# Expert stage of a fused perceiver kernel: sums copied to the output ahead of the last scatter, a narrower 16-bit table, an earlier plan, and a reordered middle stage

## The chip, the cores and the metric

The kernel is one program on one core of a Trainium2 chip. The metric is the device time of one execution in microseconds; lower is better. Times are medians of three executions. A change of 0.2% is about what such a measurement can tell from no change.

## The reference, cut to what matters

The input is x (32 sequences of 32 tokens, 1024 tokens of width 512) and a context of 32 x 257 rows of width 384. Six residual layers follow each other: a cross attention, an attention, a low-rank expert layer, a second cross attention, an attention without softmax, and a mixture of experts. The last one is what most of the change touches:

```python
# _L1_ffn_ref, per token t of 1024, 8 experts, 2 chosen
probs = softmax(x @ router_w.T)
top_w, top_idx = top_k(probs, 2); top_w /= sum(top_w)
g, u = x @ wg[e].T, x @ wu[e].T          # 512 -> 1024
out[t] = sum over the chosen e of  top_w * ((silu(g) * u) @ wd[e].T)
return x + out
```

## The kernel before

The program runs six stages one after the other, each a function with its own block of code for every engine and a barrier of all engines behind it: `latents`, `cross0`, `middle`, `cross1`, `poly`, `experts`. Every product of matrices is three 16-bit matmuls (lines 106 to 108: high by high, high by low, low by high), so most operands exist as a high and a low half. ScalarE writes the high half, VectorE or GpSimd the low one.

**middle** (attention and low-rank experts) walks 8 tiles of 128 tokens through 11 slots of a software pipeline. In slot s the lanes are t = s (output projection, residual, norm a, q/k/v), b = s-1 (softmax and attention, norm b), q = s-2 (gates, low-rank product, norm q) and last = s-3 (next stage's query). The order on each engine is written out by hand in its loop over s, and an engine works strictly in that order. The steps used below: `residual_o(t)` adds the projection to X and takes statistics (L1351 to L1346); `power` on GpSimd makes the reciprocal root (L1309, L1311); `scale` on ScalarE writes the normed row (L1496); `bias_o(t+1)` on GpSimd adds a row of biases to the next tile of X (L1314); `turned_high`, `turned_low` copy a transposed tile into halves (L1500, L1356); `soft`, `soft_exp`, `soft_scale`, `soft_high`, `soft_low` are the softmax of b (L1376 to L1392); `gates`, `gates_end` and `down` are q's gates and the scaled low-rank row dg (L1168 to L1194, L1413).

**cross1** starts with four fills on GpSimd (L1762, L1764). `sig.begin` raises counters at a loop's start so that the first pass finds its waits met; here it gives the counter d_xlo on which TensorE's first `keys` waits.

**experts** first works out a plan on all partitions alike: how many tokens each expert has, how many tiles of 128 (`tiles`, cast into `plan`), and from it a table of tiles by tokens. The table has TABLE = 34 columns (MOST = 24 possible tiles, 8, and 2). VectorE makes `past`, `inside`, three planes of `entries` and the one-hot `lane`; TensorE multiplies them into PSUM in 16 matmuls; VectorE turns the result into `fromtab`, `totab` and `gtab` (row to read, row to add into, weight). GpSimd gathers the first tile's rows, TensorE turns them (L2864), and the walk over the experts begins.

In the walk each engine reads two numbers of the plan per expert (`number`, L2579: its tiles and its first tile) and branches. Per tile TensorE makes four groups of gate and up products (pGU), turns the next tile's rows, and makes the down product (pY) of 24 matmuls. The run of the profile has 21 tiles: 2, 3, 3, 2, 3, 3, 3, 2 per expert. Expert weights come as 12 pieces of 1024 columns through a ring of 12 buffers. ScalarE writes a piece's high half (L2805), VectorE its low half (`split`, L2663), and the split's counter e_wlo lets SyncE load the next expert's piece into the buffer and lets TensorE start an expert once 12 are there. During an expert's first two tiles the next expert's pieces are split, 6 per tile: 2 ahead of the groups and one after each group.

A tile's result is weighted (`outputs`) and added by GpSimd's indirect transfer into the scratch tensor `sums` in DRAM one tile later. At the end the last result is scattered, its landing awaited, and `sums` is copied to the output.

## Time and profile before

| | before |
|---|---|
| median of three executions | 1804.37 us (1803.74 to 1806.03) |
| the profiled execution, its own time | 1802.4 us |
| its span, first to last instruction | 1800.7 us |
| mean granted clock of TensorE | 0.94 |
| TensorE, VectorE, ScalarE, GpSimd busy | 87%, 70%, 55%, 38% |

The span is what the profiler sees; 1.7 us of the execution's own time lie around it. Where a row names idle time, it is the time in which that engine did nothing just ahead of that instruction, and the name behind the arrow is who ended it. A granted clock of 1.00 is 2.4 GHz for TensorE, 0.50 is 1.2 GHz.

### The profile page before, as it was taken

Reading aid. Unit: us, or ns where it says so; the run is one execution under the profiler, and the core shown is the slowest. Engines: PE = TensorE matmul, PEld = TensorE weight load, DVE = VectorE, ACT = ScalarE, POOL = GpSimd, SP = SyncE. Lnnn points to the kernel's source line nnn. Section 1 sums busy time; section 2 is a strip of 40 time slices with the busy share of each in tenths; the row PEclk is TensorE's granted clock in tenths of the full one; section 3 lists DMA queues with packets and bytes.
Section 4 is the critical chain, followed back from the end, with each engine's and each line's share of the span. In section 5 each row is a group of like instructions: output and inputs, shape, how many; then the busy total and the mean of one; then the engine's idle time right before and its main releaser. Section 6 shows DMA issues by size and latency. Waiting matters only on the chain. (4 is left out here: it accounts for less than half of the span.)

```text
span 1800.7 us, 43529 instructions
## 1 busy us (share of the span) xinstructions
PE 1569.4 (87%) x16191; PEld 1125.5 (63%) x16191; DVE 1255.2 (70%) x2853; ACT 985.1 (55%) x2210; POOL 675.8 (38%) x796
## 2 busy tenths in 40 slices
PE   6968999999857886799999999599992699989996
PEld 3535777777645665577777777245551577777875
DVE  7858998999745777588888887577775754454431
ACT  4547887888633443366666666333333455565541
POOL 4557777777511110212211121245552223332332
PEclk9979999999978998799999999699995799999998
DMA  6111011111140000011110113401002775565422
GB/s 225 45 58 36 28 46 46 46 46 45 34 170 1 2 1 1 19 35 35 35 35 26 35 35 149 149 1 36 13 13 91 220 205 142 145 188 154 119 38 67
DMA packets 50105, 126.95 MB, mean 70 GB/s; under 512 B 6913, under 2 KB 19553, under 8 KB 49889
## 3 DMA queue, kind: packets, MB, share of 16 engines
q1 hardware_dynamic: 44914, 112.64, 19.4%
q0 software_dynamic: 5008, 11.80, 3.4%
q8 instruction: 123, 2.02, 0.5%
q14 instruction: 60, 0.49, 0.1%
HBM read 110.83 MB, written 15.68 MB: 70 GB/s over the span
## 5 line engine op out<-in xcount | busy, mean ns | idle before, releaser
L106 PE MATMUL e_pGU<-XT,WB 128*128 128x128 f16 x1344 | 232.1, 222 | 18.1 <-issue 9.0
L107 PE MATMUL e_pGU<-XT,WB 128*128 128x128 f16 x1344 | 231.9, 222 | 1.1 <-issue 1.1
L108 PE MATMUL e_pGU<-XT,WB 128*128 128x128 f16 x1344 | 231.8, 222 | 0.0
L2663 DVE SCALAR_TENSOR_TENSOR WB<-raw,WB 128x1024 f16<-128x1024 f32 x96 | 115.5, 1223 | 86.0 <-ACT WB L2805 85.9
L106 PEld LDWEIGHTS e_pGU<-XT,WB 128*128 128x128 f16 x1344 | 133.6, 99 | 23.3 <-issue 21.8
L107 PEld LDWEIGHTS e_pGU<-XT,WB 128*128 128x128 f16 x1344 | 133.6, 99 | 1.5
L108 PEld LDWEIGHTS e_pGU<-XT,WB 128*128 128x128 f16 x1344 | 133.6, 99 | 1.3 <-issue 1.3
L2646 POOL TENSOR_TENSOR XT<-e_mf,XT 128x256 f16<-128x256 f32 x84 | 56.2, 669 | 173.6 <-ACT XT L2819 173.6
L1780 POOL TENSOR_TENSOR XT<-dzo,XT 128x128 f32 (+1 forms) x32 | 13.7, 427 | 283.8 <-ACT XT L1921 283.8
L715 POOL TENSOR_TENSOR crn<-css,mhalf 128x8 f32<-128x8 f32 x64 | 108.6, 1697 | 5.3
L2805 ACT ACTIVATE WB<-raw 128x1024 f16<-128x1024 f32 x96 | 97.9, 1044 | 13.5 <-PE e_pY L108 12.5
L2779 DVE SCALAR_TENSOR_TENSOR e_mf<-e_pGU,e_sg 128x256 f32<-128x256 f32 x84 | 35.4, 421 | 84.4 <-ACT e_sg L2817 81.9
L1908 ACT ACTIVATE dpr<-dpS,dnm 128x257 f32<-128x257 f32 x128 | 59.0, 474 | 39.7 <-DVE dnm L1819 39.7
L106 PE MATMUL cpK<-W,cLT 128*128 128x512 f16 x192 | 74.0, 386 | 1.0 <-POOL cLT L704 1.0
L2819 ACT ACTIVATE XT<-e_mf 128x256 f16<-128x256 f32 x84 | 35.0, 417 | 72.0 <-DVE e_mf L2779 72.0
L107 PE MATMUL cpK<-W,cLT 128*128 128x512 f16 x192 | 74.0, 386 | 0.0
L108 PE MATMUL cpK<-W,cLT 128*128 128x512 f16 x192 | 73.9, 385 | 0.0
L106 PE MATMUL cpP<-cPT,raw 128*128 128x128 f16 x384 | 69.2, 222 | 4.8 <-DVE raw L810 2.5
L106 PE MATMUL pl_bM<-W,pl_LT 128*128 128x512 f16 x160 | 61.4, 384 | 9.7 <-DVE pl_LT L2226 9.7
L107 PE MATMUL cpP<-cPT,raw 128*128 128x128 f16 x384 | 68.6, 221 | 0.0
L108 PE MATMUL cpP<-cPT,raw 128*128 128x128 f16 x384 | 68.5, 221 | 0.0
L2817 ACT ACTIVATE e_sg<-e_pGU 128x256 f32<-128x256 f32 x84 | 31.6, 377 | 63.3 <-PE e_pGU L108 62.3
(581 smaller groups left out, 5809.5 us busy)
## 6 DMA issues: line engine op xcount, KB each, us to landing
raw<-in_WE SPq DMA_DIRECT2D x96, 512.0 KB, 4.8
raw<-in_W SPq DMA_DIRECT2D x37, 512.0 KB, 7.5
ctxin<-in_ctx SPq DMA_DIRECT2D x32, 384.0 KB, 3.3
ctxin<-in_ctxT SPq DMA_DIRECT2D x32, 384.0 KB
cv<-vlat SPq DMA_DIRECT2D x32, 96.0 KB
X<-in_x SPq DMA_DIRECT2D x8, 256.0 KB, 8.6
vlat<-vl SPq DMA_DIRECT2D x8, 256.0 KB, 2.0
dv<-vrem SPq DMA_DIRECT2D x128, 0.8 KB
```

The source lines that it names most:

```text
L106: pe.matmul(out, lh, rh, start=first, stop=False, skip_group_check=shared)
L107: pe.matmul(out, lh, rl, start=False, stop=False, skip_group_check=shared)
L108: return pe.matmul(out, ll, rh, start=False, stop=last, skip_group_check=shared)
L715: pool.tensor_tensor(rn[i][:, :], ss[i][:, :], mhalf[:, 0:H0], ALU.pow).then_inc(sig[f"c0_rn{i}"], 1)
L1780: pool.tensor_tensor(dst[:, 1, :, :], zo[:, :, :], dst[:, 0, :, :], ALU.subtract).then_inc(sig["d_olo"], 1)
L1908: act.activation(pr[:, g, :], pS[:, g, 0:SC], ACT.Exp, bias=nm[:, g:g + 1], scale=SCALE, accum_out=rsum[:, g:g + 1]).then_inc(sig["d_exp"], 1)
L2646: pool.tensor_tensor(mT[:, 1, 2 * g:2 * g + 2, :], mf[g % 2][:, :].rearrange("p (a n) -> p a n", a=2), mT[:, 0, 2 * g:2 * g + 2, :], ALU.s ...
L2663: dve.scalar_tensor_tensor(WB[w][:, 1, a], ring[n][:, :], WS, WB[w][:, 0, a], ALU.mult, ALU.subtract)\
L2779: dve.scalar_tensor_tensor(mf[g % 2][:, :], pGU[g % 2][:, 2 * T:4 * T], 1.0 / WS, sg[g % 2][:, :], ALU.mult, ALU.mult)\
L2805: act.activation(WB[w][:, 0, a], ring[n][:, :], ACT.Copy, scale=WS).then_inc(sig["e_whi"], 1)
L2817: act.activation(sg[g % 2][:, :], pGU[g % 2][:, 0:2 * T], ACT.Silu, scale=1.0 / WS).then_inc(sig["e_sg"], 1)
L2819: act.activation(mT[:, 0, 2 * g:2 * g + 2, :], mf[g % 2][:, :].rearrange("p (a n) -> p a n", a=2), ACT.Copy)\
```

## The change

It does seven things: (1) in middle, VectorE's `residual_o` moves two steps ahead and `soft_scale` behind `turned_low`, ScalarE's `turned_high` moves ahead of `soft_exp`, and GpSimd's `bias_o` moves behind the slot's three `power` calls; (2) in cross1 the begin of two counters moves ahead of the fills; (3) the table has 26 columns and its operands are 16-bit; (4) of the first expert's splits on VectorE, 4 move from ahead of the plan and 3 from ahead of the table's result to behind it; (5) TensorE starts the first gate product after 8 pieces, and the other 4 are split inside the first tile; (6) TensorE reads all 16 numbers of the plan ahead of the table; (7) `sums` is copied to the output once every scatter but the last has landed, and the last goes into the output itself, with rows past the end skipped.

```diff
@@ middle, GpSimd
                 if t is not None:
                     power("a", t)
-                    if t + 1 < NT:
-                        bias_o(t + 1)
                 if b is not None:
                     power("b", b)
                 if q is not None:
                     power("q", q)
+                if t is not None and t + 1 < NT:
+                    bias_o(t + 1)
@@ middle, VectorE
                 if q is not None:
                     turned_low("b", q, bT1, LTb)
+                if t is not None:
+                    residual_o(t)
                 if last is not None:
                     turned_low("q", last, bT0, LTq)
...
                 if b is not None:
                     value_low(b)
-                if t is not None:
-                    residual_o(t)
...
                     soft(b)
-                    soft_scale(b)
                 if q is not None:
                     gates_end(sig, dve, "m_g", q, gate[:, :, :], gwork)
                 if t is not None:
                     turned_low("a", t, bT0, LTa)
                 if b is not None:
+                    soft_scale(b)
                     soft_low(b)
@@ middle, ScalarE
-                if b is not None:
-                    soft_exp(b)
                 if t is not None:
                     turned_high("a", t, bT0, LTa)
                 if b is not None:
+                    soft_exp(b)
                     soft_high(b)
@@ cross1, GpSimd
+            sig.begin(pool, "d_olo", "d_xlo")
             for u in range(2):
                 pool.memset(qbd[u][:, :, :, :], 0.0).then_inc(sig["d_const"], 1)
...
-            sig.begin(pool, "d_olo", "d_xlo")
@@ experts
+    GUP = 2 * CK * INTER // PW
+    USED = MOST + 2
...
-                here, ahead = number(eng, e, SLOTS), number(eng, e + E1, MOST)
+                here, ahead = known[e] if known else (number(eng, e, SLOTS), number(eng, e + E1, MOST))
@@ experts, SyncE
+            sp.wait_ge(sig["e_plan"], 1)
+            total = number(sp, 2 * E1, MOST)
+            sp.wait_ge(sig["e_put"], (total + 1) * 16)
+            sp.dma_start(st["out"], sums[0:TOK, :]).then_inc(sig["e_out"], 16)
             sp.wait_ge(sig["e_end"], 1)
-            sp.dma_start(st["out"], sums[0:TOK, :]).then_inc(sig["e_out"], 16)
-            sp.wait_ge(sig["e_out"], 16)
@@ experts, GpSimd
+            pool.wait_ge(sig["e_out"], 16)
             pool.wait_ge(sig["e_y"], total + 1)
             sig.passed(pool, "pool")
-            scatter()
-            pool.wait_ge(sig["e_put"], (total + 2) * 16)
+            pool.indirect_dma_start(st["out"], bass.IndirectOffsetOnAxis(ap=torow[:, 0:1], axis=0), yo[:, :], None, compute_op=ALU.add,
+                                    bounds_check=TOK - 1, oob_is_err=False).then_inc(sig["e_last"], 16)
+            pool.wait_ge(sig["e_last"], 16)
@@ experts, VectorE
-            for n in range(4):
-                split(0, 0, n)
             dve.wait_ge(sig["e_counted"], 1)
...
-            for n in range(4, 8):
-                split(0, 0, n)
+            split(0, 0, 0)
             dve.wait_ge(sig["e_tabled"], 1)
...
+                coming = owed(e, w, pieces) + [(e + 1, 1 - w, n) for n in pieces]
+                for piece in coming[:LATE]:
+                    split(*piece)
...
+                    for piece in coming[LATE + g:LATE + g + 1]:
+                        split(*piece)
+                for piece in coming[LATE + GROUPS:]:
+                    split(*piece)
+
+            def owed(e, w, pieces):
+                return [(e, w, n) for n in range(GUP, PIECES)] if e == 0 and 0 in pieces else []
...
-            for n in range(8, PIECES):
+            for n in range(1, 6):
                 split(0, 0, n)
             dve.wait_ge(sig["e_turned"], 1)
             dve.tensor_copy(xg[:, 1, :, :], pX[1][:, 0:CK * T].rearrange("p (k n) -> p k n", k=CK)).then_inc(sig["e_xlo"], 1)
+            for n in range(6, GUP):
+                split(0, 0, n)
@@ experts, TensorE
+            pe.wait_ge(sig["e_plan"], 1)
+            known = [(number(pe, e, SLOTS), number(pe, e + E1, MOST)) for e in range(E1)]
             pe.wait_ge(sig["e_plans"], 1)
             pe.wait_ge(sig["e_entries"], 3)
...
-                pe.wait_ge(sig["e_wlo"], e * PIECES + PIECES)
+                pe.wait_ge(sig["e_wlo"], e * PIECES + (PIECES if e else GUP))
...
                 pe.wait_ge(sig["e_y"], j + 1)
+                if not e:
+                    pe.wait_ge(sig["e_wlo"], PIECES)
...
-            walk_experts(pe, tile)
+            walk_experts(pe, tile, None, known)
```

VectorE in a full slot of middle, from the value row to the gates' first step (the lines with no sign stand in both kernels):

```order
 L1366 SCALAR_TENSOR_TENSOR mid_zt<-mid_V,mrows 128x512
 L1356 TENSOR_TENSOR mid_LTb<-mid_T,mid_LTb 128x512
-L1356 TENSOR_TENSOR mid_LTq<-mid_T,mid_LTq 128x512
-L1370 TENSOR_TENSOR mid_v<-mid_zt,mid_v 128x512
 L1351 SCALAR_TENSOR_TENSOR X<-mid_O,X 128x512
 L1340 BN_STATS mid_ast<-X 128x6
 L1344 BN_AGGR mid_amv<-mid_ast 128x2
 L1346 TENSOR_SCALAR mid_amv<-mid_amv 128x1
+L1356 TENSOR_TENSOR mid_LTq<-mid_T,mid_LTq 128x512
+L1370 TENSOR_TENSOR mid_v<-mid_zt,mid_v 128x512
```

The residual and its three statistics now stand ahead of the low halves of LTq and v. On GpSimd, two slots of middle:

```order
-L1314 TENSOR_TENSOR X<-X,mrows 128x512
 L1309 TENSOR_TENSOR mid_brs<-mid_bmv,mhalf 128x1
 L1311 TENSOR_SCALAR mid_brs<-mid_brs,mid_bmv 128x1
 L1309 TENSOR_TENSOR mid_qrs<-mid_qmv,mhalf 128x1
 L1311 TENSOR_SCALAR mid_qrs<-mid_qrs,mid_qmv 128x1
+L1314 TENSOR_TENSOR X<-X,mrows 128x512
 L1309 TENSOR_TENSOR mid_ars<-mid_amv,mhalf 128x1
 L1311 TENSOR_SCALAR mid_ars<-mid_ars,mid_amv 128x1
-L1314 TENSOR_TENSOR X<-X,mrows 128x512
 L1309 TENSOR_TENSOR mid_brs<-mid_bmv,mhalf 128x1
 L1311 TENSOR_SCALAR mid_brs<-mid_brs,mid_bmv 128x1
```

The bias add of 128x512 now follows the reciprocal root of q, the last of the slot, where it followed that of a. VectorE at the start of experts, from the last small step ahead of the plan to the transposed rows; before:

```order
L2690 TENSOR_SCALAR r_own<-r_own 128x1
L2663 SCALAR_TENSOR_TENSOR WB<-raw,WB 128x1024 x4
L2694 COPY e_count<-e_pR 128x8
...
L2731 TENSOR_TENSOR e_entries<-e_inside,e_values 128x16x34 x3
L2734 TENSOR_TENSOR XT<-r_count,e_within 128x2048
L2663 SCALAR_TENSOR_TENSOR WB<-raw,WB 128x1024 x4
L2740 COPY e_token<-e_pR 128x34
...
L2752 SCALAR_TENSOR_TENSOR e_gtab<-e_pR,e_gtab 128x34
L2663 SCALAR_TENSOR_TENSOR WB<-raw,WB 128x1024 x4
L2793 COPY XT<-e_pX 128x512
```

and with the change:

```order
L2697 TENSOR_SCALAR r_own<-r_own 128x1
L2699 COPY e_count<-e_pR 128x8
...
L2736 TENSOR_TENSOR e_entries<-e_inside,e_values 128x16x26 x3
L2741 TENSOR_TENSOR XT<-e_numbers,e_within 128x1024 x2
L2669 SCALAR_TENSOR_TENSOR WB<-raw,WB 128x1024
L2747 COPY e_token<-e_pR 128x26
...
L2759 SCALAR_TENSOR_TENSOR e_gtab<-e_pR,e_gtab 128x26
L2669 SCALAR_TENSOR_TENSOR WB<-raw,WB 128x1024 x5
L2806 COPY XT<-e_pX 128x512
L2669 SCALAR_TENSOR_TENSOR WB<-raw,WB 128x1024 x2
```

The splits (SCALAR_TENSOR_TENSOR on WB) stood 4, 4 and 4 around the count and the table, and stand 1, 5 and 2 now; 4 more are inside the first tile. TensorE at the same place, from the counts to the first gate product; before:

```order
L2850 MATMUL e_pR<-e_sel,r_ones 128x8 x8
L2856 MATMUL e_pR<-e_entries,XT 128x102 x16
L2864 MATMUL e_pX<-r_ident,e_xrow 128x128 x8
L2579 TENSOR_LOAD e_plan
L2579 ISA x2
...
L2588 COMPARE_AND_BRANCH
L2871 REGISTER_ALU
L2875 ISA
L106 MATMUL e_pGU<-XT,WB 128x128
```

and with the change (the load and the row behind it stand 16 times):

```order
L2865 MATMUL e_pR<-e_sel,r_ones 128x8 x8
L2581 TENSOR_LOAD e_plan
L2581 ISA x2
...
L2874 MATMUL e_pR<-e_entries,XT 128x78 x16
L2881 MATMUL e_pX<-r_ident,e_xrow 128x128 x8
L2590 COMPARE_AND_BRANCH
L2888 REGISTER_ALU
L2892 ISA
L106 MATMUL e_pGU<-XT,WB 128x128
```

The loads of the plan have moved from behind the transposed rows to ahead of the table's matmuls, 16 in place of 2, and every later expert starts without its pair.

## Rows read from the trace of the kernel before

**Rows 1.** Timeline, VectorE, one slot of the middle: start us, duration us, then [idle before <-releaser].
```profile
607.63 0.68 DVE L1351 SCALAR_TENSOR_TENSOR X<-mid_O,X 128x512 f32<-128x512 f32 x1
...
610.80 0.94 DVE L1178 TENSOR_SCALAR mg_sel<-mg_rank 128x8 f32<-128x8 f32 x1
...
613.46 0.16 DVE L1384 RECIPROCAL mid_rs<-mid_rs 128x1 f32<-128x1 f32 x1 [0.48 <-ACT mid_ex L1513]
...
618.66 0.29 DVE L1418 TENSOR_TENSOR mid_dT<-mid_K,mid_dT 128x128 f16<-128x128 f32 x1 [0.48 <-ACT mid_dT L1528]
...
626.49 1.13 DVE L1361 SCALAR_TENSOR_TENSOR mid_kT<-mid_K,vecs,mid_kT 128x128 f16<-128x128 f32 x4 [2.90 <-ACT mid_kT L1505]
...
629.92 0.68 DVE L1351 SCALAR_TENSOR_TENSOR X<-mid_O,X 128x512 f32<-128x512 f32 x1
```

**Rows 2.** Timeline, VectorE, the first slot without a bias add.
```profile
677.70 0.17 DVE L1178 TENSOR_SCALAR mg_sel<-mg_rank 128x8 f32<-128x8 f32 x1
```

**Rows 3.** Timeline, GpSimd and ScalarE, same slot as rows 1.
```profile
610.46 1.26 POOL L1314 TENSOR_TENSOR X<-X,mrows 128x512 f32<-128x512 f32 x1
...
613.93 0.98 ACT L1520 ACTIVATE mid_aB<-mid_ex 32x32 f16<-32x32 f32 x4
```

**Rows 4.** Timeline, start of cross1: GpSimd, TensorE.
```profile
735.23 1.84 POOL L1762 MEMSET dq<- 128x1024 f16 x2 [6.26 <-POOLq L145]
...
738.59 0.39 PE L106 MATMUL dpK<-KL,W 128*128 128x256 f16 x1 [7.48 <-POOLq L90]
```

**Rows 5.** Timeline, start of experts: VectorE and TensorE.
```profile
1388.91 4.62 DVE L2663 SCALAR_TENSOR_TENSOR WB<-raw,WB 128x1024 f16<-128x1024 f32 x4
...
1393.45 0.16 DVE L2694 COPY e_count<-e_pR 128x8 f32<-128x8 f32 x1
...
1394.74 0.18 DVE L2708 CAST e_plan<-e_tiles 128x17 int32<-128x17 f32 x1
...
1400.31 2.28 DVE L2734 TENSOR_TENSOR XT<-r_count,e_within 128x2048 f16<-128x2048 f32 x1
...
1402.74 1.52 PE L2856 MATMUL e_pR<-e_entries,XT 128*128 128x102 f16 x16 [15.55 <-DVE XT L2734]
...
1407.06 0.19 DVE L2740 COPY e_token<-e_pR 128x34 f32<-128x34 f32 x1
...
1408.69 4.63 DVE L2663 SCALAR_TENSOR_TENSOR WB<-raw,WB 128x1024 f16<-128x1024 f32 x4
...
1415.57 0.28 PE L106 MATMUL e_pGU<-XT,WB 128*128 128x128 f16 x1 [1.14 <-ACT XT L2836]
```

**Rows 6.** Line of number(), window 1749:1753: count, ns min/median/max, first and last start.
```profile
L2579 PEldq TENSOR_LOAD <-e_plan x2: 301/304/307, 1749.9 to 1750.5; - x2
```

**Rows 7.** Waits of TensorE, 1415:1800: total us, times, longest us.
```profile
PE e_pGU L106 <- issue: 9.0, 5, 1.9
PE e_pGU L106 <- DVE WB L2663: 8.0, 2, 4.1
```

**Rows 8.** Windows in experts: us, busy of PE, PEld, DVE, ACT, POOL, granted clock, DMA share, GB/s.
```profile
1454.60:1459.00 4.40, 4.39 (x51) 4.40 (x52) 0.91 (x1) 0.00 (x0) 1.25 (x1) 0.63 0.86 210
1507.30:1510.00 2.70, 2.70 (x49) 2.70 (x50) 1.55 (x2) 1.39 (x2) 1.89 (x1) 1.00 0.38 67
1595.20:1603.00 7.80, 6.60 (x76) 6.45 (x77) 0.88 (x2) 0.84 (x3) 0.79 (x1) 0.61 0.70 195
```

**Rows 9.** End of the kernel, timeline: GpSimd, GpSimd, SyncE's queue.
```profile
1769.73 1.60 POOL L2629 DMA_INDIRECT sums<-e_yo,e_torow  x1 [3.94 <-DVE e_yo L2767]
...
1786.11 1.57 POOL L2629 DMA_INDIRECT sums<-e_yo,e_torow  x1 [5.18 <-DVE e_yo L2767]
...
1791.07 0.60 SPq L2615 DMA_DIRECT2D out_y<-sums  x1
```

**Rows 10.** Transfers on out_y, then on sums from 1440 on: issue to landing.
```profile
DMA to landing us min/median/max: 8.1/8.1/8.1
...
DMA to landing us min/median/max: 4.8/6.9/9.2
```

More of the change, by code:

```diff
@@ L2726, in _ @@
             dve.wait_ge(sig["e_spot"], 7)
-            dve.tensor_scalar(within[:, :], within[:, :], float(T + 1), None, ALU.add).then_inc(sig["e_spot"], 1)
+            dve.tensor_scalar(within16[:, :], within[:, :], float(T + 1), None, ALU.add).then_inc(sig["e_spot"], 1)
             dve.wait_ge(sig["e_inside"], 1)
-            dve.wait_ge(sig["e_values"], 5)
+            dve.wait_ge(sig["e_values"], 6)
             for i in range(3):
-                dve.tensor_tensor(entries[:, :, i, :], inside[:, :, :], values[:, i, :].unsqueeze(2).broadcast_to([P, PAIRS, TABLE]), ALU.mult)\
+                dve.tensor_tensor(entries[:, :, i, :], inside[:, :, :], values[:, i, :].unsqueeze(2).broadcast_to([P, PAIRS, USED]), ALU.mult)\
@@ L2732, in _ @@
                    .then_inc(sig["e_entries"], 1)
             dve.wait_ge(sig["e_spot"], 8)
-            dve.tensor_tensor(lane[:, :, :], slots[:, 0:T].unsqueeze(1).broadcast_to([P, PAIRS, T]),
-                              within[:, :].unsqueeze(2).broadcast_to([P, PAIRS, T]), ALU.is_equal).then_inc(sig["e_lane"], 1)
-            for n in range(4, 8):
-                split(0, 0, n)
+            for i in range(2):
+                half = slice(i * NT, (i + 1) * NT)
+                dve.tensor_tensor(lane[:, half, :], numbers16[:, :].unsqueeze(1).broadcast_to([P, NT, T]),
+                                  within16[:, half].unsqueeze(2).broadcast_to([P, NT, T]), ALU.is_equal).then_inc(sig["e_lane"], 1)
@@ L2738, in _ @@
+            split(0, 0, 0)
             dve.wait_ge(sig["e_tabled"], 1)
[L2739 to L2740 removed]
+            tab = lambda n: pR[1][0:T, n * USED:(n + 1) * USED]
+            used = slice(0, USED)
+            dve.tensor_copy(token[0:T, used], tab(0)).then_inc(sig["e_tab"], 1)
             dve.wait_ge(sig["e_tab"], 1)
[L2742 removed]
@@ L2773, in tile @@
                 outputs(j)
-                for n in pieces[:LATE]:
-                    split(e + 1, 1 - w, n)
+                coming = owed(e, w, pieces) + [(e + 1, 1 - w, n) for n in pieces]
+                for piece in coming[:LATE]:
+                    split(*piece)
                 for g in range(GROUPS):
@@ L2782, in tile @@
                         turned_low(j + 1)
-                    if pieces:
-                        split(e + 1, 1 - w, pieces[LATE + g])
+                    for piece in coming[LATE + g:LATE + g + 1]:
[4 more added lines that the diff above has]
+                return [(e, w, n) for n in range(GUP, PIECES)] if e == 0 and 0 in pieces else []
             def between(j, e, w, pieces):
-                for n in pieces:
-                    split(e + 1, 1 - w, n)
-            for n in range(8, PIECES):
+                for piece in owed(e, w, pieces) + [(e + 1, 1 - w, n) for n in pieces]:
+                    split(*piece)
+            for n in range(1, 6):
                 split(0, 0, n)
```

40 lines of the change are left out of this document (20 added, 20 removed).

## Prediction

> **What bounds the kernel now.** I read the table of engines first (TensorE 87% busy, clock 0.94 in the mean), then the waits of each engine stage by stage, then timelines at the places that the diff touches. TensorE bounds most of experts: its idle time there is short and lies in few places. Between the tiles of one expert it does not stop; at changes of expert it does, 9.0 us in five waits that no semaphore explains and 8.0 us in two of about 4 us that are put down to VectorE's split [rows 7]. Behind each of the two long ones the clock has fallen, behind a short one it has not [rows 8]. At the start of experts TensorE stands still for 15.55 us ahead of the table's matmuls, and at the end a copy to the output follows the last scatter [rows 5, 9, 10]. In middle it is another engine: over one slot of 22.29 us VectorE has only four pauses, 0.48, 0.48, 2.90 and one hidden in a long `mg_sel`, so the slot is VectorE's work plus its pauses [rows 1].
>
> **A, middle: −2.5 us.** `mg_sel` (8 elements a partition) takes 0.94 us in this slot and 0.17 in the first slot without a bias add [rows 1, 2]. GpSimd's bias add runs from 610.46 to 611.72, and `mg_sel` ends at 611.74 [rows 1, 3]: VectorE was held by GpSimd for 0.77 us. This hang-over is what the moved `bias_o` takes away; at its new place, behind the power of q, VectorE is either in work that reads PSUM or in its 2.90 pause.
> The Trainium skill has the same thing as a rule (SBUF — State Buffer, section "Who interferes with whom"): VectorE and GpSimd share a pair of ports under an exclusive lock, and a `tensor_scalar` from SBUF can need it. By that rule the add may hold another VectorE step at its new place and A would lose 0.8 us a slot; the trace shows the hold once a slot, in the one place.
> The two pauses of 0.48 wait for ScalarE's exp and for its dT [rows 1]. Both engines' lists are turned so that the turned tile comes first and the softmax later; the exp is then early enough, and dT is ready while VectorE writes LTa's low half: −0.96. New waits: `soft_low` now stands right behind `soft_scale`, and in between ScalarE needs 0.98 us for its four copies [rows 3] plus a hand-over (I take 0.07): +1.05. `residual_o` stands closer to TensorE's projection: +0.1. Together −0.77 −0.96 +1.05 +0.1 = −0.6 a slot, in the five slots that have gates and a bias add: −3.0. Two slots at the end have the gates without an add and lose instead, 0.2 and 0.3: −2.5. Bounds: if the pauses only move and the wait of 1.05 comes on top, 5 × (−0.77 + 1.05) = 1.4, or about +1 with the pauses partly gone; if `soft_low` finds its copies done, −4.5 or somewhat more.
>
> **B, start of cross1: −2.9 us.** TensorE's first keys start at 738.59 after a wait for GpSimd's queue; the queue does its four fills first, from 735.23 on [rows 4]. With the begin ahead of them, TensorE can start at 735.2 plus what VectorE's own begin needs (0.4, an estimate): 738.6 − 735.6 = 3.0, less 0.1. Nobody needs the fills before the products of the queries. Bounds 0 (another counter is as late) and −3.4.
>
> **C, start of experts: −3.3 us.** Ahead of the plan 4 splits (4.62 us for x4) are gone, so `e_plan` is cast 4.4 us earlier, at 1390.4 instead of 1394.8 [rows 5]; 0.2 goes to a small step that is added there. TensorE then makes its 16 loads. The trace has two of 0.30 us, one behind the other at a distance of 0.6 [rows 6]. 16 × 0.63 = 10.1: they end near 1400.7. VectorE's `past`, `inside`, entries and lane, in order from the cast, took 1394.9 to 1402.6, 7.7 us with one product as one instruction; with 26 of 34 columns about 7, so VectorE is ready near 1397.5 and TensorE's loads are what comes last. The table's matmuls take 1.52 × 78/102 = 1.2, and the first copy out of them starts at 1402.1 instead of 1407.06. From there before: 8.5 us to the first gate product, with four splits of 4.63 [rows 5]. After: 1.6 for the small tables, then five splits, the 0.4 copy of the low rows and two more, 7 × 1.16 = 8.1 since a start now wants 8 pieces and one is done earlier: 10.1. So 1402.1 + 10.1 = 1412.2, against 1415.57. Bounds: if the loads cost a third of that, VectorE decides, the copy starts at 1398.4 and the gate product at 1408.5: −7.1. If a load costs 0.75 it is −1.4, at 0.85 it is nothing.
> The Trainium skill has a price for such a load too (Runtime: NRT & Kernel Launch, section "Instruction fetch mechanics"): about 200 ns a register, from HBM. By it the 16 take 3.2 us, VectorE decides and C is the bound of −7.1. The trace's row has 0.30 for one and 0.6 from one start to the next, here from a tile on the chip, so the two differ; I go by the distance of the starts, and the cheap loads are a rival.
> The four splits owed inside the first tile (4 × 1.16 = 4.6) make VectorE late by about 1 us once, of which TensorE feels an estimated 0.4, counted with D.
>
> **D, changes of expert: −11.2 us.** The five short waits come to 9.0, 1.8 each [rows 7]. Two loads at a distance of 0.6 are 1.2 of it; the rest I take for the start-up of the emptied queue of instructions behind them. Changes of tile within an expert have no loads and no wait, so I leave 0.15 each: −8.2. The two long ones, 8.0 together, stand behind experts of 2 tiles. Their rows name VectorE's split, but its line is that of pieces whose split had ended before TensorE ran dry, so I hold it for a label; the loads stand there too, and I take off the same 1.7 each: −3.4. The other 2.3 each stand, of a cause that no row shows. With +0.4 from C's owed splits: −8.2 −3.4 +0.4 = −11.2. Bounds −6.3 (of each of the seven waits only 0.9 goes) and −13 (half of the 2.3 goes too).
>
> **The clock: −4.2 us.** After the 3.9 us wait the clock was 0.63 over 4.40 us: 4.40 × 0.37 = 1.6 lost. After the 4.1 us wait it was 0.61 over 7.80 us with TensorE busy 6.60: 6.60 × 0.39 = 2.6. After a 1.9 us wait it stayed 1.00 [rows 7, 8]. The new waits of 2.3 are nearer to 1.9 than to 3.9, so I take the loss as gone. Bounds 0 and −4.2.
>
> **E, the end: −8.1 us.** The copy takes 8.1 us from issue to landing [rows 10] and now needs only the last but one scatter: issued 1769.73, landed 6.9 later (9.2 at worst), 8.1 for the copy: it lands at 1784.7 (1787.0). The last scatter is issued at 1786.11 [rows 9]: hidden, at worst 1 us of waiting. The last scatter itself costs what it did; a bounds check adds at most some tenths. Bounds −7 and −8.3.
>
> **Sum.** −2.5 −2.9 −3.3 −11.2 −4.2 −8.1 = −32.2. The profiled execution took 1802.4, so it would take 1770.2; against the median of 1804.37 it is 1772.2. I give the latter.
>
> **Rivals.**
> R1, TensorE still halts for long at changes of expert: the 2.3 us are enough to drop the clock, and 0.47 instead of 0.15 stays at each short wait: +4.2 for the clock, 5 × 0.32 = 1.6, and 2 × 0.35 more at the long ones: +6.5, 1778.7. For it: the long waits are not the loads' doing. Against it: 1.9 did no harm to the clock. The same section of the Trainium skill (Runtime: NRT & Kernel Launch) says that a taken branch out of the fetched pages stalls the engine; an expert of 2 tiles branches past a third, and by it the 2.3 would stay. No row here shows a fetch.
> R2, loads are cheap in a row, VectorE bounds the table: 1768.5, the C bound of −7.1. For it: a load shows 0.30. Against: the second starts 0.6 after the first.
> R3, middle gives nothing, since VectorE only waits elsewhere: 1774.7. For it: `soft_low`'s new wait is as big as what goes.
> R4, slower: the narrow start leaves VectorE and ScalarE late in every tile (owed pieces, late weights ring), and TensorE starts each of the 21 tiles after a wait, like the one ahead of the clock's second fall, and pays 2.5 us at half clock: 21 × 2.5 = 52, 1824.7. It decides from 13 tiles on (32.2 / 2.5). Against it: VectorE has pauses of over 1 us in each tile, and within an expert TensorE shows none.
>
> **How the numbers follow.** Forecast 0.42 (its own range 1770 to 1776), R1 0.27, R2 0.12, R3 0.10, R4 0.03, mixtures 0.06. R2 is the low end, with a part of D's bound: 1767. R1 with a middle that gives nothing is 1781.2: high end 1781. A measurement of this kernel tells 0.2% (3.6 us) from no change. All cases but R4 lie more than 20 us below: faster 0.95, same 0.02 (R4 in some 12 to 14 tiles), slower 0.03 (R4).
>
> **What the changed profile would show.** A: `mg_sel` 0.17 in every slot, slots 21.7 apart, a wait for ScalarE's mid_aB ahead of `soft_low`; wrong if another VectorE step is as long as the bias add. B: TensorE's first keys 3 us closer to the fills' start, ahead of their end. C: 16 loads at 0.6 end after `lane`; a wait for VectorE there instead means R2. D: no wait over 0.3 at five changes of expert, two of 2.3; the clock at the window behind them 1.00, or 0.6 by R1. E: the copy issued inside the last tile, a scatter as the last transfer. What would make it wrong above all is a wait at changes of expert that has nothing to do with the loads, since D and the clock are half of the sum.

## The result and the profile after

The changed kernel took 1786.32 us (median, 1783.35 to 1787.33), the one before in the same runs 1804.05; the ratio is 0.9899 (0.9882 to 0.9916), 18 us less. The forecast was 1772.2 with a range from 1767 to 1781: the direction was right, the size was not, and the time lies 5 us above the range. It had given 0.95 to the cases of more than 20 us less. Ratios leave out executions in a slower state of the chip, of which there was one (1867.14 us, of y_bias below).

The profiled execution has a span of 1785.6 us against 1800.7, so 15.1 of it are to be found. Each line below is the shift of one mark between the two timelines; the marks are VectorE's first step on X in middle (517.39 and 516.75), its last one there (719.67, 717.64), its first fill of experts (1384.13, 1377.59), the first gate product (1415.57, 1406.30), the end of the last matmul (1784.47, 1773.21) and the end of the span.

| stretch | forecast | measured |
|---|---|---|
| ahead of the first step on X (not changed) | 0 | −0.6 |
| A, middle | −2.5 | −1.4 |
| B, from middle's last step on X to experts | −2.9 | −4.5 |
| C, start of experts to the first gate product | −3.3 | −2.7 |
| D and clock, first gate product to last matmul | −15.4 | −2.0 |
| E, last matmul to the end | −8.1 | −3.8 |

A, B and C together are what they were said to be (−8.6 for −8.7), in part by luck: A lacks 1.9 us that the last tile of middle lost, B has 1.6 from a stretch that was not changed, and the two nearly cancel. Nearly all that is missing lies in the walk over the experts (13.4 us), the rest at the end (4.3 us).

**Middle.** Timeline of VectorE in one slot of the changed kernel (compare [rows 1]):

```profile
583.54 0.69 DVE L1351 SCALAR_TENSOR_TENSOR X<-mid_O,X 128x512 f32<-128x512 f32 x1
...
587.91 0.17 DVE L1178 TENSOR_SCALAR mg_sel<-mg_rank 128x8 f32<-128x8 f32 x1
...
592.11 0.83 DVE L1392 TENSOR_TENSOR mid_aB<-mid_ex,mid_aB 32x32 f16<-32x32 f32 x4 [1.05 <-ACT mid_aB L1520]
...
602.68 1.13 DVE L1361 SCALAR_TENSOR_TENSOR mid_kT<-mid_K,vecs,mid_kT 128x128 f16<-128x128 f32 x4 [2.90 <-ACT mid_kT L1505]
...
605.10 0.69 DVE L1351 SCALAR_TENSOR_TENSOR X<-mid_O,X 128x512 f32<-128x512 f32 x1
```

`mg_sel` is at 0.17, both waits of 0.48 are gone, a new one of 1.05 stands ahead of `soft_low`, and the slot is 21.56 us instead of 22.29. Up to the step on X of the last tile but one (706.34 and 702.41) the stage is 3.3 us shorter. From there to the last one it is 1.9 us longer, in windows before and after (busy times of PE, PEld, DVE, ACT, POOL, then the granted clock):

```profile
706.34:719.67 13.33, 8.40 (x86) 6.75 (x86) 7.62 (x28) 4.28 (x10) 1.63 (x4) 0.72 0.00 1
```

```profile
702.41:717.64 15.23, 9.85 (x86) 7.79 (x86) 7.65 (x28) 4.28 (x10) 1.62 (x4) 0.72 0.00 1
```

The same 86 matmuls keep TensorE busy for 9.85 us instead of 8.40: the stretch at 1.2 GHz falls on more of them. What moved it onto them no run here tells.

**Start of cross1 and of experts.** Timelines of TensorE and VectorE at the places of [rows 4, 5]:

```profile
733.66 0.37 PE L106 MATMUL dpK<-KL,W 128*128 128x256 f16 x1 [4.46 <-POOLq L90]
...
1383.79 0.18 DVE L2713 CAST e_plan<-e_tiles 128x17 int32<-128x17 f32 x1
...
1390.63 1.22 DVE L2669 SCALAR_TENSOR_TENSOR WB<-raw,WB 128x1024 f16<-128x1024 f32 x1
...
1396.08 0.19 DVE L2747 COPY e_token<-e_pR 128x26 f32<-128x26 f32 x1 [4.23 <-PE e_pR L2874]
```

and TensorE's loads in the same stretch (line view of `number`: count, ns, first and last start):

```profile
L2581 PEldq TENSOR_LOAD <-e_plan x16: 295/300/496, 1384.0 to 1393.9; - x16
```

TensorE's first keys wait 4.46 us instead of 7.48, which is 3.0 of B's 4.5. Between the keys and experts, where nothing was changed, it is 1.6 us shorter too; the two kernels y_begin and y_bias below, with that stretch as it was, are 1.6 and 1.3 shorter there, so I don't put this down to the change. Sixteen loads in 9.9 us from first to last start, 0.66 apart, end some 4 us behind VectorE's last product ahead of the table: the loads decide, as the forecast took it.

**Changes of expert.** Waits of TensorE in the changed kernel (total, times, longest; compare [rows 7]):

```profile
PE e_pGU L106 <- issue: 13.3, 7, 6.8
PE e_pGU L106 <- DVE WB L2669: 4.8, 1, 4.8
PE e_pGU L108 <- issue: 1.6, 1, 1.6
```

The 4.8 is the wait for the first gate product. The seven changes of expert still cost 13.3 us. The two behind experts of 2 tiles have gone from 3.9 and 4.1 to 3.7 and 6.8, the five short ones from 9.0 together to 2.8; and one of 1.6 is new, in the midst of the fourth expert's first gate products. The kernel before has such a second stop too, a few products behind the jump into its fifth expert, and it is gone from there:

```profile
1597.32 0.27 PE L107 MATMUL e_pGU<-XT,WB 128*128 128x128 f16 x1 [1.13 <-issue]
```

What these are the profile of the kernel before could have told: TensorE's branches at the two ends of an expert, in the line view, first before (L2593 stands behind the second tile, L2595 behind the third), then after (L2595 and L2597):

```profile
L2593 PEldq COMPARE_BRANCH  x7: 68/68/4176, 1448.8 to 1731.6; - x7
...
L2595 PEldq COMPARE_BRANCH  x5: 3396/3446/3622, 1501.9 to 1746.4; - x5
```

```profile
L2597 PEldq COMPARE_BRANCH  x5: 3373/3494/3809, 1493.9 to 1736.5; - x5
...
L2595 PEldq COMPARE_BRANCH  x1: 4651/4651/4651, 1441.6 to 1441.6; - x1
...
L2595 PEldq COMPARE_BRANCH  x1: 3888/3888/3888, 1580.8 to 1580.8; - x1
```

A branch that falls through takes 0.07 us, a taken one over the code of tiles that the expert doesn't have 3.4 to 4.7. Behind the third tile it starts 3.5 us ahead of the end of TensorE's last matmul, which still stands in the queue (1493.9 and 1497.4 for the first), and so it is nearly hidden; behind a second tile it starts 1.5 and 1.9 us ahead (1441.6 and 1443.0, 1580.8 and 1582.7) and shows. The eighth expert's, which leaves the walk, takes 3.6 us before and 6.3 after, beside the work at the end that the other engines still have.

The 6.8 us has a second part. The branch at 1580.8 is over at 1584.7; two instructions of the new place follow at once, the third only at 1589.3 (line views of L2888 and L2890, then the page's row of the queue that brings instructions, and that queue in the window from 1586 to 1588):

```profile
L2888 PEldq ALU_OP  x1: 36/36/36, 1584.9 to 1584.9; - x1
...
L2890 PEldq EVENT_SEMAPHORE  x1: 51/51/51, 1589.3 to 1589.3; - x1
```

```profile
q8 instruction: 123, 2.02, 0.5%
```

```profile
q8 instruction: 1, 0.02, 3.0%
```

2.02 MB in 123 packets are 16 KB each. One of them lies between the two instructions, which fits that TensorE had come to the end of a block of code just behind the jump and waited for the next; x_pad below tests it. The Trainium skill (Runtime: NRT & Kernel Launch, "Instruction fetch mechanics") says that code comes in 16 KB blocks of 256 instructions, fetched ahead in sequence, and that a taken branch out of the fetched ones stalls; the packets of 16 KB and the branches of 3.4 us and more agree. The forecast cited the rule for a rival and left it at "No row here shows a fetch"; the rows above do.

**Clock.** Windows of 5 us behind the two long stops (columns as in [rows 8]; the clock is the third number from the end):

```profile
1446.70:1451.70 5.00, 4.99 (x64) 4.99 (x65) 1.85 (x3) 0.48 (x2) 1.71 (x1) 0.69 0.81 206
1589.50:1594.50 5.00, 4.94 (x59) 4.96 (x60) 0.00 (x0) 0.36 (x1) 0.00 (x0) 0.64 0.71 215
```

It fell both times, to 1.2 GHz for a part of each window: 5 × 0.31 + 5 × 0.36 = 3.4 us lost. Of the 4.2 that were to come back 0.8 did.

**The end.** The chain that ended last, its last links, and GpSimd's drain at the end of its block (line view of L2543):

```profile
1758.47 6.00 DMA sums<-e_yo,e_torow
1764.49 10.09 DMA out_y<-sums
1774.81 0.82 issue
1775.64 1.57 POOL out_y L2658
```

```profile
L2543 POOLq DRAIN  x1: 3743/3743/3743, 1780.5 to 1780.5; - x1
```

The copy took 10.1 us instead of 8.1 (8.4 to 11.4 in the other kernels with the early copy, 8.0 in y_copy), the last scatter waited for it (2.4 us from TensorE's end to its issue, 1.6 before), and behind its landing GpSimd drains for 3.74 us before the block can end. The kernel before has the same drain, beside the copy:

```profile
L2542 POOLq DRAIN  x1: 3746/3746/3746, 1791.1 to 1791.1; - x1
```

### The profile page after: what moved, and what is told of

It is laid out like the page before. It is cut to its first block and busy times, and to the rows that moved or that the text cites. A ratio compares the mean times of both kernels' runs of the same rounds, so it can differ in the third digit from the quotient of the medians.

```text
span 1785.6 us, 43534 instructions
## 1 busy us (share of the span) xinstructions
PE 1568.9 (88%) x16191; PEld 1125.6 (63%) x16191; DVE 1248.6 (70%) x2855; ACT 985.8 (55%) x2210; POOL 680.9 (38%) x796
## 3 DMA queue, kind: packets, MB, share of 16 engines
q8 instruction: 123, 2.02, 0.5%
## 5 line engine op out<-in xcount | busy, mean ns | idle before, releaser
L106 PE MATMUL e_pGU<-XT,WB 128*128 128x128 f16 x1344 | 232.2, 222 | 18.7 <-issue 13.3
L1780 POOL TENSOR_TENSOR XT<-dzo,XT 128x128 f32 (+1 forms) x32 | 13.7, 427 | 283.1 <-ACT XT L1920 283.1
```

Source lines behind the costliest of these rows:

```text
L106: pe.matmul(out, lh, rh, start=first, stop=False, skip_group_check=shared)
L1780: pool.tensor_tensor(dst[:, 1, :, :], zo[:, :, :], dst[:, 0, :, :], ALU.subtract).then_inc(sig["d_olo"], 1)
```

## The experiments

Two theories stood against each other for the walk. **F**: what is left at changes of expert is instructions being fetched, its size set by which branches are taken and by where their targets lie in the 16 KB blocks. **G**: the stops come from splits or other data. The kernel before had medians of 1801.2 to 1804.1 in the four sets of runs, so parts of a few us are compared in the timelines, counted from a mark of the same run. Even there the walk over the experts of one and the same code on TensorE differs by 3 us between profiles (366.9 in the changed kernel, 369.6 in x_drain, 369.9 in y_copy), as the clock falls once more behind the stop in the fourth expert or not; so single stops weigh more than the sum.

**x_three: no body for a fourth tile on TensorE.** The third body becomes a loop that also takes a fourth tile and more.

```diff
                 with eng.If(here > 2):
+                    if known:
+                        with eng.Fori(0, here - 2) as s:
+                            tile(ahead + s + 2, e, w, ())
+                        return
```

> The changed kernel, but TensorE's code of an expert has three bodies of a tile in place of four: the third is a loop whose end is the number of tiles read from the plan, so that an expert of 3 tiles runs straight through and one of 2 tiles jumps over one body. Theory F (what is left at changes of expert is instructions being fetched after a taken branch): the five short stops of TensorE (2.8 us together) and the 1.6 us stop just behind one of them go to nearly nothing, the two long stops (3.7 and 6.8) keep one fetch, 2.3 to 3.7 each; in all 5 to 9 us less than the changed kernel, 1777 to 1781. Rival G (the stops come from splits or other data): not changed, 1786.

Measured 1777.32, ratio 0.9860 (0.9844 to 0.9877). From the first gate product to the last matmul it is 358.8 us, 8.1 less than in the changed kernel. TensorE's waits between 1405 and the end, and its branches behind the third tile:

```profile
PE e_pGU L106 <- issue: 6.6, 2, 3.4
...
PE e_pGU L107 <- issue: 1.3, 1, 1.3
```

```profile
L2597 PEldq COMPARE_BRANCH  x5: 72/73/73, 1491.7 to 1728.2; - x5
```

The five short stops are gone, not smaller: the branch at the end of an expert of 3 tiles falls through and takes 0.07. Nothing in the data was changed, so G is out for them, and for the stop of 1.6 in the fourth expert, which went too. The two long stops keep one fetch each (3.1 and 3.4 behind branches of 4.1 and 4.5), and a second one of 1.3 stands behind the latter, some 50 instructions in.

**x_pad: 8 instructions more ahead of the walk.**

```diff
             turn()
+            for _ in range(8):
+                sig.passed(pe, "pe")
             walk_experts(pe, tile, None, known)
```

> The changed kernel with 8 small instructions (counter increments) more on TensorE ahead of the walk over the experts, at a place where it waits anyway. Theory F: the code behind them moves by 8 instructions against the 16 KB blocks in which instructions are fetched, so the target of the jump into the fifth expert stands at the start of a block and not two instructions ahead of its end: the 6.8 us stop becomes one like the other long one, 2.3 to 3.7 us, 3 to 4.5 us less in all (1782 to 1783); the 1.6 us stop inside the first gate products of the fourth expert stays or grows by some tenths. Rival G: no stop changes, 1786.

Measured 1783.07, ratio 0.9889 (0.9872 to 0.9905); from the first gate product to the last matmul 363.9 us, 3.0 less. The stop into the fifth expert:

```profile
1588.81 0.23 PE L106 MATMUL e_pGU<-XT,WB 128*128 128x128 f16 x1 [2.44 <-issue]
```

2.44 us where the changed kernel has 6.84, by eight small instructions placed 180 us earlier. The branch ahead of it takes 3.88, as in the changed kernel, but the third instruction behind it now follows at once, at 1588.6 (it came 4.5 us after the second one there):

```profile
L2890 PEldq EVENT_SEMAPHORE  x1: 51/51/51, 1588.6 to 1588.6; - x1
```

The stop inside the fourth expert is 1.77 (was 1.62), and a small one of 0.68 is new inside the third, so not all of the 4.4 us remain. The ratios, 0.9889 and 0.9899, have overlapping intervals: it is the stop that shows it, not the time. The clock fell behind the 1.77 instead; behind the 2.44 it stayed at 2.4 GHz:

```profile
1588.84:1593.84 5.00, 5.00 (x91) 5.00 (x92) 2.41 (x3) 2.53 (x4) 2.69 (x3) 1.00 0.86 222
```

**x_loads: TensorE's loads back at each expert.**

```diff
-            known = [(number(pe, e, SLOTS), number(pe, e + E1, MOST)) for e in range(E1)]
...
-            walk_experts(pe, tile, None, known)
+            walk_experts(pe, tile)
```

> The changed kernel, but TensorE reads its two numbers per expert at the expert, as before, and none ahead of the table. The table's matmuls then start when VectorE is ready, about 3 us earlier; each of the seven changes of expert gets two loads back, 1.2 us each (8.5). Sum: 5 us more, 1791. Under theory F the code also moves against the 16 KB blocks, by 6 instructions an expert, which can take 2 to 4 us off the stop of 6.8.

Measured 1784.60, ratio 0.9903 (0.9887 to 0.9920): the changed kernel's time within what the runs tell, not 5 us more. Ahead of the walk the gain is larger than said: the first gate product starts 4.3 us earlier (24.4 us behind VectorE's first fill of experts, instead of 28.7). The five short stops are 1.7 to 2.1, 1.4 more each. The first long one is 4.9, 1.3 more; the second 4.5, 2.3 less although it has its loads back, and the stop of 1.6 in the fourth expert is gone; by F that is because the code of an expert is longer by the loads and the ends of the blocks fall elsewhere. From the first gate product to the last matmul it is 371.2 us, not 366.9: 4.3 more, against 4.3 less ahead of it. Reading all 16 numbers ahead, in one row, gave what it cost and no more.

**x_drain: SyncE awaits the last landing.**

```diff
             sp.wait_ge(sig["e_end"], 1)
+            sp.wait_ge(sig["e_last"], 16)
...
-            pool.wait_ge(sig["e_last"], 16)
```

> The changed kernel, but the landing of the last scatter is awaited by SyncE, so that GpSimd goes to the end of its block right after issuing it. If the drain of GpSimd at the end of the block (3.74 us in the changed kernel, behind the landing) is a fixed cost that needs nothing of the landing, it lies beside the 4.7 us landing and the kernel takes 3.5 to 3.7 us less, 1782.6. If the drain itself waits for the transfer, nothing changes: 1786.

Measured 1783.99, ratio 0.9887 (0.9866 to 0.9907). GpSimd's drain:

```profile
L2543 POOLq DRAIN  x1: 6662/6662/6662, 1776.8 to 1776.8; - x1
```

It starts with the scatter's issue, not 4.9 us behind it, and takes 6.66 us. The scatter lands 4.7 us after its issue, so the drain ends 1.9 us behind the landing. In z_two below, with the same end, the landing takes 4.0 us and the drain is as much shorter:

```profile
L2543 POOLq DRAIN  x1: 5958/5958/5958, 1759.5 to 1759.5; - x1
```

Again it ends 1.9 us behind the landing (and so it does in z_one and z_hint, 6.80 and 6.67 us with landings of 4.8 and 4.7). So the drain does wait for the transfer, which was the rival, but then needs 1.9 us more where it takes 3.74 if it starts only behind the landing. From the scatter's issue to the end of the span it is 8.0 us instead of 10.0: 2 us, about half of what was expected. From the last matmul to the end only 0.8 of it shows (11.6 us instead of 12.4), since the copy took 11.4 us in this run and the scatter was issued later.

**y_copy: the end as it was.** The last scatter goes into `sums`, and the copy follows.

```diff
-            sp.wait_ge(sig["e_put"], (total + 1) * 16)
-            sp.dma_start(st["out"], sums[0:TOK, :]).then_inc(sig["e_out"], 16)
             sp.wait_ge(sig["e_end"], 1)
+            sp.dma_start(st["out"], sums[0:TOK, :]).then_inc(sig["e_out"], 16)
+            sp.wait_ge(sig["e_out"], 16)
```

> The changed kernel with the end as it was: the last scatter goes into sums, and the copy to the output follows its landing. From the end of TensorE's last matmul to the end of the span the changed kernel took 12.4 us and the one before 16.2. Theory (the early copy hides 8.1 us but brings 3.7 us of drain on GpSimd into the open and makes the last scatter wait 0.8 us for the copy's landing): 16.2 us again, the drain beside the copy, 1790. Rival (the drain is a result of the bounds check or of the scatter into the output): the drain is gone or short here and the tail under 16.

Measured 1790.19, ratio 0.9937 (0.9914 to 0.9960), 16.2 us from the last matmul to the end (1772.12 to 1788.3), and the drain is there, hidden:

```profile
L2543 POOLq DRAIN  x1: 3746/3746/3746, 1778.8 to 1778.8; - x1
```

So the early copy is worth 3.8 us, and the drain belongs to the end of GpSimd's block, not to the new scatter. The ratios are further apart (0.9937 and 0.9899, 6.8 us), because the walk took 369.9 us in this run and not 366.9, with its end changed but nothing on TensorE: a stop of 2.1 us stands in the fourth expert, and the clock fell behind it (window of 5 us):

```profile
1547.65:1552.65 5.00, 5.00 (x61) 5.00 (x61) 0.74 (x2) 1.75 (x3) 0.67 (x1) 0.66 0.85 246
```

**y_wide: the first gate product after all 12 pieces.**

```diff
-    GUP = 2 * CK * INTER // PW
+    GUP = PIECES
```

> The changed kernel, but the first gate product waits for all 12 pieces, as before, and nothing is owed inside the first tile. It starts 4 splits later (4.6 us). Theory (the narrow start costs 1 us inside the first expert, a 0.4 us stop and a longer stretch at half clock): the first expert's two tiles take 35.5 to 36 us from first product to last, not 36.7, so 3.6 us more in all, 1789.5. Rival (the 1.6 us come from fetched instructions, not from splits): the first expert stays at 36.7, 1791.

Measured 1786.76, ratio 0.9918 (0.9895 to 0.9940) where the changed kernel's is 0.9899: 3.4 us more by the ratios, whose intervals overlap. The timeline is clearer. The first gate product starts 4.5 us later, counted from the stage before, and the first expert takes 35.1 us instead of 36.7, which is what it took before. So the narrow start is worth 2.9 us, and the splits, not fetches, make the first expert longer. In the changed kernel 0.4 of the 1.6 is a stop that VectorE ends, and 0.6 lies in the first gate products (13.7 instead of 13.2 us), which start at 1.2 GHz and stay there longer. Their first 7 us, in the changed kernel and here (the clock is the third number from the end):

```profile
1406.30:1413.30 7.00, 7.00 (x75) 7.00 (x76) 4.33 (x5) 1.36 (x4) 2.87 (x3) 0.58 1.03 384
```

```profile
1408.56:1415.56 7.00, 7.00 (x85) 7.00 (x86) 3.44 (x4) 1.36 (x3) 4.11 (x3) 0.66 1.02 408
```

The wait ahead of them is not what does it: it is 4.8 us there and 9.2 here. For the other 0.6 I have no row.

**y_bias: the kernel before with the bias add moved, nothing else.**

```diff
                 if t is not None:
                     power("a", t)
-                    if t + 1 < NT:
-                        bias_o(t + 1)
...
                     power("q", q)
+                if t is not None and t + 1 < NT:
+                    bias_o(t + 1)
```

> The kernel before with one edit: GpSimd's bias add in middle stands behind the slot's three power steps. Theory (the hold is by GpSimd's add, and at the new place it meets an idle VectorE): the step mg_sel falls from 0.94 to 0.17 us in all slots, the two waits of 0.48 stay, the slot goes from 22.29 to 21.5 us in five slots, 3.9 us less in middle, 1798. Rival (the hold only moves to another VectorE step, or a pause takes it up): slot 22.3, 1802.

Measured 1799.03, ratio 0.9979 (0.9964 to 0.9994). One slot:

```profile
603.99 0.68 DVE L1351 SCALAR_TENSOR_TENSOR X<-mid_O,X 128x512 f32<-128x512 f32 x1
...
607.16 0.17 DVE L1178 TENSOR_SCALAR mg_sel<-mg_rank 128x8 f32<-128x8 f32 x1
...
609.04 0.16 DVE L1384 RECIPROCAL mid_rs<-mid_rs 128x1 f32<-128x1 f32 x1 [0.48 <-ACT mid_ex L1513]
...
625.52 0.68 DVE L1351 SCALAR_TENSOR_TENSOR X<-mid_O,X 128x512 f32<-128x512 f32 x1
```

The slot is 21.53 with both waits still there (0.48 ahead of this reciprocal and 0.49 ahead of dT). The whole gain of A is this one line; the reordering on VectorE and ScalarE trades 0.96 for 1.05. From the first to the last step on X the stage takes 199.1 us here, 200.9 in the changed kernel and 202.3 before: without the reordering it is 1.8 us faster still. The last tile's 1.9 us are lost here too, so they don't come from the reordering.

**y_begin: the kernel before with the counters' begin moved, executed once.**

```diff
+            sig.begin(pool, "d_olo", "d_xlo")
             for u in range(2):
                 pool.memset(qbd[u][:, :, :, :], 0.0).then_inc(sig["d_const"], 1)
...
-            sig.begin(pool, "d_olo", "d_xlo")
             walk(pool, body, None, lambda: out_low(B - 1))
```

> The kernel before with the begin of the two counters of cross1 ahead of the four fills, nothing else. Theory: TensorE's first keys start 2.9 us earlier, counted from the last matmul of middle (its wait of 7.5 goes to 4.6), and the stage ends about as much earlier. Rival: a later wait gives it back, and the stage's last instructions keep their distance from middle's end.

```profile
735.20 0.37 PE L106 MATMUL dpK<-KL,W 128*128 128x256 f16 x1 [4.46 <-POOLq L90]
```

Measured 1798.68, one execution. The wait is 4.46 instead of 7.48, 3.0 less, and the stretch from middle's last step on X to experts is 4.5 us shorter (719.17 to 1379.14, against 719.67 to 1384.13), so nothing takes it back. y_bias, with nothing changed in that stretch, is 1.2 us shorter there too, so what goes beyond 3.0 is not shown to be the edit's.

**z_one: put together, with executed padding.** Three bodies, SyncE at the end, 10 loads ahead of the table and 6 behind its matmuls, and:

```diff
+            for _ in range(60):
+                sig.passed(pe, "pe")
             pe.wait_ge(sig["e_plan"], 1)
```

> Put together: the changed kernel with TensorE's third tile of an expert as a loop (three bodies), SyncE awaiting the last scatter's landing, 10 of TensorE's 16 loads ahead of the table and 6 behind its matmuls, and 60 small instructions on TensorE ahead of the plan, where it waits, which move the code of the experts by 60 instructions against the 16 KB blocks. Theory F: against the kernel with three bodies alone (1777.3) the table comes 3 us earlier, the end is 2 us shorter, and the second stop behind the jump into the fifth expert (1.3 us, and half clock around it) is gone: 1770 to 1772. Rival (the loads behind the table delay the first tile, and padding does nothing): 1775.

Measured 1772.10, ratio 0.9834 (0.9812 to 0.9856). The stop behind the jump into the fifth expert is 2.8 with no second one, but a second one of 1.27 now stands behind the jump into the second expert: the boundary was only moved from one target to the other. And the padding was not free: 60 increments took 9 us (0.15 each), longer than the wait that was to hide them, so the table's matmuls came 1.6 us later than in x_three, not 3 us earlier.

**z_two: padding that is jumped over.**

```diff
             turn()
+            with pe.If(known[0][0] < 1):
+                for _ in range(108):
+                    sig.passed(pe, "pe")
             walk_experts(pe, tile, None, known)
```

> Put together again: three bodies on TensorE, SyncE awaiting the last landing, 10 loads ahead of the table and 6 behind it, and in place of the 60 executed instructions 108 that are jumped over, in front of the walk, where TensorE waits for splits. Theory F: the first gate product comes 4 us earlier than in the kernel with three bodies alone (counted from the last matmul of the stage before), no second stop stands behind either of the two jumps, each keeps one stop of about 3; 2 us less at the end. 1777.3 - 4 - 2.5 - 2 = 1769, or 1768. Rival (the position in the 16 KB blocks has nothing to do with the second stops): one of 1.3 us stays at the fifth or at the second expert, 1771.

Measured 1767.70, ratio 0.9810 (0.9796 to 0.9824). No second stop stands behind either jump; those left are 3.86 and 3.36, at branches of 4.83 and 4.48 us. The first gate product comes 24.7 us behind VectorE's first fill of experts, 3.9 earlier than in x_three.

**z_hint: the coming branch is announced.** In front of an expert's second tile TensorE is told the address of the branch over the third and whether it will be taken. The branch itself is written in another form for it.

```diff
                     with eng.If(here > s):
+                        if known and s:
+                            loc = eng.mark_branch_hint_location(eng.to_reg(here > 2))
                         tile(ahead + s, e, w, pieces)
...
+                    eng.br_lt(eng.to_reg(here), 3, on_true=past, on_false=more).branch_hint(loc)
```

Measured 1759.63 (1759.21 to 1763.55), ratio 0.9771 (0.9757 to 0.9784). The branch into the second expert in the line view, first in z_two and then here, then the two stops in the timeline here and a window behind the first:

```profile
L2595 PEldq COMPARE_BRANCH  x1: 4828/4828/4828, 1435.5 to 1435.5; - x1
```

```profile
L2600 PEldq COMPARE_BRANCH  x1: 484/484/484, 1437.9 to 1437.9; - x1
```

```profile
1440.06 0.23 PE L107 MATMUL e_pGU<-XT,WB 128*128 128x128 f16 x1 [0.65 <-DVE WB L2681]
...
1571.99 0.23 PE L107 MATMUL e_pGU<-XT,WB 128*128 128x128 f16 x1 [0.54 <-DVE WB L2681]
```

```profile
1440.01:1445.00 4.99, 4.94 (x89) 4.95 (x90) 3.77 (x7) 3.53 (x4) 2.69 (x2) 1.00 0.62 167
```

The two branches are 0.48 and 0.46 us, the stops 0.65 and 0.54, and the clock stays at 2.4 GHz. The walk over the experts takes 348.0 us instead of z_two's 357.0. The queue of instructions shows the fetch: one packet starts inside z_two's branch into the fifth expert (1572.9 to 1577.3), and none inside the same one here: from 1569.8 to 1570.4 only the queue of ordinary transfers, q1, has packets:

```profile
q8 instruction: 1, 0.02, 1.6%
```

```profile
q1 hardware_dynamic: 22, 0.09, 64.9%
```

No kernel has the new form of the branch without the announcement. But the eighth expert's branch, which leaves the walk, has both and still takes 3.76 us (3.78 in z_two), so the form alone does not make a branch short; why the announcement did nothing there is open:

```profile
L2600 PEldq COMPARE_BRANCH  x1: 3761/3761/3761, 1748.6 to 1748.6; - x1
```

This kernel is 42 us faster than the one before in its runs (1801.24), and by the ratios 1.3% faster than the change studied (0.9771 against 0.9899).

## Why the prediction was wrong

- **What bounds the kernel**: right. TensorE was the bound of experts, VectorE the ring of middle.
- **A**: right in its parts; the hold went (0.94 to 0.17) and the new wait is the 1.05 forecast. In size it was −3.3 up to the last tile but one and −1.4 with the last, whose 1.9 us at a lower clock the sum did not have. The Trainium skill's rule on the shared ports (SBUF — State Buffer, "Who interferes with whom") agrees with y_bias, where moving the add alone takes `mg_sel` from 0.94 to 0.17; that the add would catch another VectorE step at its new place did not come true.
- **B**: right, 3.0 less of waiting at the first keys for −2.9; the stretch behind it was another 1.6 shorter, not shown to be of the edit.
- **C**: right, −2.7 for −3.3. The loads decided, at 0.66 each instead of 0.63. R2, cheap loads, is out.
- **D, the step that failed**: "The other 2.3 each stand, of a cause that no row shows" and "I leave 0.15 each". The cause was in the trace, in branches of 3.4 to 4.2 us on TensorE's queue, which the wait view shows only as "issue" or under another engine's name. Taking the loads away took 1.2 off each short stop, as costed, but not the rest, since a branch of 3.5 us starts 3.5 us ahead of the end and then still shows: 2.8 stayed instead of 0.75. The long stops were to be 2.3 each. The first is 3.7: its loads went, but its branch takes 4.65 us instead of 4.02 and starts 1.5 us ahead of the last matmul's end instead of 1.9 (y_wide, with 3.85 and 1.9, has a stop of 2.4). The second is 6.8: without a block's end two instructions behind the target it is 2.4 (x_pad), near the 2.3. That end cost 4.4 us, and another some 50 instructions behind the jump into the fourth expert 1.6, while the 1.1 of the kernel before went, which the forecast had missed ("within an expert TensorE shows none"); where the blocks end it had not asked. Together +2.1 +1.6 −1.1 +5.9 (10.5 instead of 4.6) of the 13.4 that are missing; the next two points bring 3.4 and 1.2, which makes 13.1. Some 5 of these us (4.4 +1.6 −1.1) are bad luck of where the code lay, the rest of D is what the branches cost wherever it lies.
- **The clock**: its condition failed with D. The stops were 3.7 and 6.8, not 2.3, and 3.4 us were lost where it had been 4.2.
- **C's owed splits**, 0.4: mis-sized. The first expert took 1.6 longer, partly at half clock (y_wide shows the 1.6; 1.0 of it has rows).
- **E**: the copy was hidden, but "the last scatter itself costs what it did" left out what stood beside the copy: a drain of 3.74 us on GpSimd, which became the path. With 0.8 of waiting for the copy, which ran 2 us longer than alone, some −3.6 is left by the terms, and −3.8 was measured.
- **R1** was the nearest rival in kind (long halts stay, clock falls) but priced them at 6.5 us; it was 13. It rested on the branch rule and was given 0.27 for want of a row that was there.

## What to carry to other kernels

Where an engine waits for "issue", or for a name that had long been done, look at its branches' own durations: a taken branch over code that isn't at hand cost 3.3 to 4.9 us here inside the walk, and whether it shows depends on how much work the engine has queued. Price an edit of such code by both the work that it removes and the jumps that it leaves, and expect a few us of luck from where the targets fall (4.4 us in x_pad); make the likely path fall through, or announce the branch (4.8 us became 0.5 at two of the three taken ones). Before a transfer at the end is hidden, look for what ends beside it.

## What was not expected of the hardware

- Eight small instructions ahead of the walk changed a stop 180 us further on from 6.84 to 2.44 us, as was expected from the boundary of a 16 KB block.
- The clock does not follow the length of a stop alone: it stayed at 2.4 GHz behind stops of 2.44 (x_pad) and 3.36 (z_two), and fell behind one of 2.43 (y_wide, the window below) and one of 1.77 (x_pad) that came 1.2 us behind another of 0.91.

```profile
1446.12:1451.12 5.00, 5.00 (x61) 5.00 (x62) 2.81 (x4) 1.31 (x3) 2.43 (x2) 0.66 0.79 204
```

- GpSimd's drain at the end of a block took 3.74 us when it began behind the landing of the last indirect transfer. When it began with that transfer's issue it ended 1.9 us behind the landing, four times out of four (5.96 to 6.80 us long).
- A counter increment on TensorE's queue took 0.15 us each in a row, 9 us for sixty.
